# Cross-attention and a two-of-eight expert layer on one core: half the tokens through 15 sorted expert tiles, the other half dense

## The reference, cut to what matters

```
x   = x + xattn(layernorm(x), ctx)            # x (4, 256, 128), ctx (4, 1601, 128), one head of 128
x   = x + ffn(layernorm(x))

# ffn, per token (4 * 256 = 1024 tokens):
scores = softmax(flat @ router_weight.T + router_bias)        # 8 experts
topk_w, topk_idx = top_k(scores, 2)
gu   = einsum('th,ehn->ten', flat, gate_up_proj) + gate_up_bias   # (1024, 8, 512)
gate = minimum(gu[..., :256], 7);  up = clip(gu[..., 256:], -7, 7)
act  = (up + 1) * gate * sigmoid(1.702 * gate)
down = einsum('tei,eih->teh', act, down_proj) + down_bias         # (1024, 8, 128)
out  = sum over the two chosen experts of topk_w * down
```

## Time and profile before

| | |
|---|---|
| median of 3 runs | 157.16 us (156.94 to 157.22) |
| the profiled execution | 156.96 us |
| span of its trace | 155.2 us |
| TensorE busy | 149.2 us, 96% of the span |
| granted TensorE clock | 1.00 throughout |
| DMA queues | 10.69 MB, nearly all in the first fifth of the span |

### The profile page before, as it was taken

One profiled execution on the slowest core, in us unless ns is written; L12 is line 12 of the kernel. 1 busy time (PEld: TensorE's weight loads), 2 busy tenths in 40 slices (PEclk: granted clock), 3 DMA queues, 4 the chain that ended last, 5 costly groups with the idle time before them and its releaser, 6 DMA issues.

```text
span 155.2 us, 3023 instructions
## 1 busy us (share of the span) xinstructions
PE 149.2 (96%) x1004; PEld 136.0 (88%) x1004; DVE 103.2 (66%) x288; ACT 100.8 (65%) x205; POOL 49.8 (32%) x49
## 2 busy tenths in 40 slices
PE   7998799999999999999999999999999999999993
PEld 7988699999999999989988888788888888887892
DVE  0668958386859595963683899957654377552773
ACT  3183878657484736468866656957788677779450
POOL 1356529243505300210067643312333321233020
PEclk9999999999999999999999999999999999999999
DMA  4979999700000000000000000000000000000022
GB/s 116 371 292 404 388 401 384 225 1 4 0 2 0 4 0 0 4 0 2 0 0 4 0 0 0 0 4 0 2 0 0 0 0 0 0 4 0 4 68 68
DMA packets 5909, 10.69 MB, mean 69 GB/s; under 512 B 380, under 2 KB 3080, under 8 KB 5896
## 3 DMA queue, kind: packets, MB, share of 16 engines
q1 hardware_dynamic: 4968, 10.00, 17.9%
q10 hardware_dynamic: 928, 0.53, 1.2%
HBM read 10.00 MB, written 0.52 MB: 68 GB/s over the span
## 4 chain that ended last, share of the span: by engine, by line
PE 78%; DVE 10%; POOL 4%; ACT 3%; issue 3%; DVEq 0%
PE T L1147 14%; PE O L1041 13%; PE S L944 11%; PE S L946 10%; PE S L945 10%; PE T L1025 6%; PE S L951 3%; POOL ex L309 2%; DVE xT L847 2%; DVE up L838 1%; PE S L1147 1%; DVE w_lo L779 1%; DVE sc L631 1%; ACT pr L419 1%; POOL rstd L287 1%
## 5 line engine op out<-in xcount | busy, mean ns | idle before, releaser
L838 DVE TENSOR_SCALAR up<-up 128x512 f32<-128x512 f32 x32 | 13.9, 434 | 24.7 <-ACT up L504 24.7
L350 POOL TENSOR_TENSOR x<-x,xn 128x512 f32<-128x512 f32 x13 | 17.3, 1331 | 38.6 <-ACT xn L524 38.6
L427 ACT ACTIVATE pT<-T 128x512 f32<-128x512 f32 (+1 forms) x32 | 15.4, 513 | 18.4 <-PE T L1025 18.4
L524 ACT ACTIVATE xn<-T,w_scaled 128x128 f32<-128x128 f32 x56 | 16.1, 374 | 17.2 <-PE T L1147 14.1
L944 PE MATMUL S<-x_hi,w_hi 128*128 128x512 f32 x64 | 26.8, 419 | 0.2 <-DVE w_lo L779 0.2
L1041 PE MATMUL O<-pT,ctx_sb 128*128 128x128 f32 (+1 forms) x208 | 25.9, 275 | 0.2 <-ACT pT L427 0.2
L945 PE MATMUL S<-x_lo,w_hi 128*128 128x512 f32 x64 | 25.3, 395 | 0.0
L946 PE MATMUL S<-x_hi,w_lo 128*128 128x512 f32 x64 | 25.3, 395 | 0.0
L1041 PEld LDWEIGHTS O<-pT,ctx_sb 128*128 128x128 f32 (+1 forms) x208 | 24.6, 192 | 0.6 <-ACT pT L427 0.5
L631 DVE TENSOR_SCALAR_CACHE_REDUCE sc<-S,clip_hi 128x400 f32<-128x400 f32 (+1 forms) x32 | 18.9, 630 | 8.7 <-PE S L946 8.5
L498 ACT ACTIVATE keysT_sb<-S,gate_bias 128x512 f32<-128x512 f32 x32 | 22.7, 708 | 1.7 <-PE S L946 1.6
(11 more groups left out here) (127 smaller groups left out, 248.4 us busy)
## 6 DMA issues: line engine op xcount, KB each, us to landing
keysT_sb<-in_ctxT SPq DMA_DIRECT2D x3, 801.0 KB, 9.9
ctx_sb<-in_ctx SPq DMA_DIRECT2D x3, 768.0 KB
gu_sb<-in_gu SPq DMA_DIRECT2D x1, 2048.0 KB, 14.9
ctx_sb<-in_ctx SPq DMA_DIRECT2D x3, 256.0 KB, 4.5
x_sb<-in_x ACTq DMA_DIRECT2D x1, 384.0 KB, 5.0
keysT_sb<-in_ctxT SPq DMA_DIRECT2D x1, 289.0 KB, 5.5
out_x<-xn SPq DMA_DIRECT2D x1, 256.0 KB, 2.3
out_x<-xn SPq DMA_DIRECT2D x2, 128.0 KB, 1.8
```

The source lines that it names most:

```text
L350: nc.gpsimd.tensor_tensor(acc, acc, y_sb[:, k % 2, :], ALU.add).then_inc(y_added, 1)
L524: ins = nc.scalar.activation(y_sb[:, k % 2, t * DIM:(t + 1) * DIM], T[k % 2][:, t * DIM:(t + 1) * DIM], ACT.Copy, scale=w_scaled[:, bass.d ...
L838: nc.vector.tensor_scalar(up[:, k % 2, ih, :], up[:, k % 2, ih, :], 2.0 * LIMIT, 1.0 - LIMIT, ALU.min, ALU.add).then_inc(up_clipped, 1)
```

## The change

Batches 2 and 3 (512 tokens) stay dense: 8 steps instead of 16. Batches 0 and 1 (512 tokens, each with two experts, so 1024 rows) are sorted by expert into tiles of 128 rows, each tile of one expert. 1024 rows are 8 tiles, and 8 experts can leave up to 7 more partly filled: 15 tiles always, whatever the routing.

- During attention, the router results of batches 0 and 1 are ranked on VectorE (`rank_experts`), TensorE counts how many rows of each expert come before each token (`count_before`, 2 and 6 small matmuls), VectorE turns that into a row number (`find_rows`), and GpSimd scatters the normalised rows to DRAM (`send_rows`, 4 indirect DMAs a batch), with the place of its result as a 129th column. The DRAM area is filled with ones first (`blank_rows`, 2.6 MB). An indirect DMA with no use for its data goes first (`first_send`).
- Behind the last attention tile's router, VectorE computes from the counts which expert each tile belongs to and where its rows start (`compare_counts`, `tile_table`). SP reads each start into a register and loads the tile (15 loads). TensorE reads each tile's expert into a register (`load_expert`).
- A tile on TensorE: one transposition, a bias product of 16 rows by 512 columns, three products of 512 columns with the rows as stationary operand, two transpositions of the activations, and two float32 matmuls of 128 columns. ScalarE does four instructions a tile (128, 256, 256, 128 columns), VectorE three (128, 256, 256). GpSimd scatters each result (`send_result`), SP brings all of them back behind the last, and VectorE adds them with their weights (`sum_results`).
- All eight experts' weights are split ahead and kept, on ScalarE (`weights_hi`) and GpSimd (`weights_lo`, 8 subtractions of 128x512), instead of on VectorE one by one. They are loaded where the transposed keys lie, in three DMAs (`expert_weights`), each waiting for its keys' last reader.
- Expert 0 of the dense half is split in two items of 256 columns: batch 2 ahead of the tiles, batch 3 behind them. The other seven follow.
- The blank operand of the first matmuls is now `ones`, 1677 columns wide instead of 128.

```
+SPARSE = [0, 1]
+DENSE = [2, 3]
+RT = len(SPARSE) * TPB
+RTOK = RT * P
+SLOTS = RT * TOP_K + EXPERTS - 1
...
+            def expert_weights(k):
+                e0, n = W_PARTS[k]
+                sp.wait_ge(keys_lo_ready, (k + 1) * NCH)
+                sp.dma_start(keysT_sb[:, k, 0:n * 2 * HIDDEN].rearrange("p (e n) -> p e n", e=n),
+                             gu[e0:e0 + n].rearrange("e h n -> h e n")).then_inc(w_in[k], 16)
...
+            sp.wait_ge(first_row_ready, 1)
+            for i in range(SLOTS):
+                at = sp.value_load(first_row[0:1, i:i + 1], min_val=0, max_val=ROWS - P)
+                if i == 0:
+                    for s in range(len(SPARSE)):
+                        sp.wait_ge(rows_sent[s], 16 * TOP_K * TPB)
+                sp.dma_start(xt[:, i, :], xs[bass.ds(at, P), :]).then_inc(xt_in[i], 16)
...
+                pool.wait_ge(pads_in, 16)
+                pool.wait_ge(first_sent, 16)
+                pool.wait_ge(payload_copied, s + 1)
+                pool.wait_ge(row_ready, s + 1)
...
+                        nc.gpsimd.indirect_dma_start(xs[:, :], bass.IndirectOffsetOnAxis(ap=row_of[:, s, k:k + 1], axis=0),
...
+            def send_result(i):
+                pool.wait_ge(y_ready, i + 1)
+                nc.gpsimd.indirect_dma_start(yb[:, :], bass.IndirectOffsetOnAxis(ap=xt[:, i, DEST:DEST + 1].bitcast(I32), axis=0),
...
+            first_send()
             root2(0)
+            copy_payload(0)
             keys_lo(3, 0)
+            weights_lo(0)
+            weights_lo(1)
+            weights_lo(2)
             keys_lo(3, 1)
+            weights_lo(3)
             root2(1)
+            copy_payload(1)
+            send_rows(0)
+            weights_lo(4)
+            weights_lo(5)
             root2(2)
+            send_rows(1)
+            weights_lo(6)
+            weights_lo(7)
             root2(3)
...
+            for k in range(-2, SLOTS + 2):
+                if 0 <= k - 2:
+                    evict(k - 2)
+                if 0 <= k - 1 < SLOTS:
+                    copy_act(k - 1)
+                if k + 2 < SLOTS:
+                    split_rows(k + 2)
+                if 0 <= k + 1 < SLOTS:
+                    silu(k + 1)
...
+            def tile_table():
+                dve.wait_ge(counted, 1)
+                link(nc.vector.tensor_reduce(tiles_of[:], full[:], AX.X, ALU.add))
+                nc.vector.tensor_scalar(gap[:], tiles_of[:, 0:EXPERTS - 1], -float(P), float(RTOK), ALU.mult, ALU.add)
+                link(nc.vector.tensor_tensor(tiles_upto[:], upto[:], tiles_of[:].unsqueeze(1).to_broadcast([P, EXPERTS - 1, EXPERTS]),
+                                             ALU.mult))
+                link(nc.vector.tensor_reduce(last_of[:], tiles_upto[:], AX.X, ALU.add))
+                shape = [P, SLOTS, EXPERTS - 1]
+                link(nc.vector.tensor_tensor(passed[:], tile_no[:].unsqueeze(2).to_broadcast(shape),
+                                             last_of[:].unsqueeze(1).to_broadcast(shape), ALU.is_ge))
+                link(nc.vector.tensor_reduce(expert_no[:], passed[:], AX.X, ALU.add))
+                link(nc.vector.tensor_tensor(passed[:], passed[:], gap[:].unsqueeze(1).to_broadcast(shape), ALU.mult))
+                link(nc.vector.tensor_reduce(skipped[:], passed[:], AX.X, ALU.add))
+                nc.vector.scalar_tensor_tensor(first_row[:], tile_no[:], float(P), skipped[:], ALU.mult,
+                                               ALU.add).then_inc(first_row_ready, 1)
+                nc.vector.tensor_scalar(expert_at[:], expert_no[:], float(P), None, ALU.mult)
+                nc.vector.tensor_scalar(bias_pick[:], expert_no[0:BIAS_ROWS, :], bias_expert[:, 0:1],
+                                        None, ALU.is_equal).then_inc(table_ready, 1)
...
-            nc.vector.memset(act_odd[:, 0:P], 0.0).then_inc(blank_ready, 1)
+            nc.vector.memset(ones[:], 1.0).then_inc(blank_ready, 1)
             nc.vector.memset(inv_sum[:, 0:1], 0.0).then_inc(pad_ready, 1)
...
+            def gate_up(i):
+                if i == 0:
+                    load_expert(0)
+                    pe.wait_ge(bias_ready, 1)
+                    pe.wait_ge(w_lo_ready, EXPERTS)
+                    pe.wait_ge(d_silu_ready, 2)
+                pe.wait_ge(xt_lo_ready, i + 1)
+                if i >= 2:
+                    pe.wait_ge(up_ready, i - 1)
+                cols = bass.ds(expert[i], P)
+                dst = GU[i % 2][:].rearrange("p (c n) -> p c n", c=WIDTH)
+                nc.tensor.matmul(GU[i % 2][:], bias_pick[:, i:i + 1].to_broadcast([BIAS_ROWS, P]), bias_parts[:],
+                                 start=True, stop=False)
+                nc.tensor.matmul(dst, xt_hi[:, i % 2, :], w_hi[:, :, cols], start=False, stop=False)
+                nc.tensor.matmul(dst, xt_hi[:, i % 2, :], w_lo[:, :, cols], start=False, stop=False)
+                nc.tensor.matmul(dst, xt_lo[:, i % 2, :], w_hi[:, :, cols], start=False, stop=True).then_inc(gu_done, 1)
+                if i + 1 < SLOTS:
+                    load_expert(i + 1)
...
+            dense_gate_up(0, 1, 0)
+            dense_gate_up(0, 1, 1)
+            for k in range(-2, SLOTS + 1):
+                if k + 2 < SLOTS:
+                    transpose_rows(k + 2)
+                if 0 <= k + 1 < SLOTS:
+                    gate_up(k + 1)
+                if 0 <= k - 1:
+                    down(k - 1)
+                if k == SLOTS - 1:
+                    dense_gate_up(1, 0, 0)
+                    dense_gate_up(1, 0, 1)
+                if 0 <= k < SLOTS:
+                    transpose_act(k)
+                if k == SLOTS - 1:
+                    dense_gate_up(1, 1, 0)
+                if k == 1:
                     transpose_x2(last)
-                    routed_bias(0)
+                if k == X2_LAST:
                     router(last)
...
+            dense_gate_up(1, 1, 1)
+            dense_gate_ups(2)
+            for e in range(EXPERTS - 2):
+                dense_down(e)
+                if e in (1, 3):
+                    routed_bias(e // 2)
+                dense_gate_ups(e + 3)
+                if e in (0, 2):
+                    transpose_weights(e // 2)
+            dense_down(EXPERTS - 2)
+            dense_down(EXPERTS - 1, tiles_apart=True)
 
```

918 lines of the change are left out of this document (591 added, 327 removed).

## The result

The changed kernel takes **168.98 us** (median of 4 runs, 168.82 to 169.37) against 157.16 before: a ratio of 1.076, 95% interval 1.074 to 1.078. I had forecast 154.8, range 150 to 162, and slower only with a chance of 0.38. The profiled execution has a span of 167.3 us where the sum gave 153.0.

What follows compares the result with a forecast made beforehand. TensorE, busy 96% of the span, was taken as the bound. Span: 155.2 - 11.0 - 1.4 + 1.3 + 0.9 + 1.1 + 5.0 + 1.4 + 0.5 = 153.0; plus 1.8 gives 154.8 us, range 150.0 to 162.0.

Steps and rivals of the forecast that it cites:

- start: Kernel start: TensorE's first record waits for the memset of the wider block of ones, +1.3 us.
- GpSimd ahead of root2(1): Attention, batch 1: weight subtractions queued before GpSimd's root make VectorE's normalisation and TensorE wait, +1.1 us, bounds 0 and 2.
- Counting: TensorE's queue: the 2 and then 6 narrow matmuls of `count_before` add 0.9 us.
- Between attention and the tiles: Between last router and first tile: TensorE idle 5.0 us for table, register read and row load, bounds 3.5 and 8.
- dense steps: Expert layer: eight of sixteen dense steps of 4.59 us go, -36.7 us.
- The sorted rows come late: Rival: batch 2 of scatters lands after SP's first register; rows 3.9 us late, 158.7 us; chance 0.09.
- The waits are smaller: Rival: start, root2, gap and tile waits each cost less than forecast, 150.8 us; chance 0.21.
- The rate of the tiles: Tile stretch: ScalarE and VectorE keep up with TensorE, waits of 0.09 us a tile, +1.4 us, bounds 0.3 and 4.5.
- Tiles: TensorE's work per tile, 1.71 us with all four 512-column products at 0.233; fifteen tiles +25.7 us.
- The clock: Rival: TensorE slows down behind its 5 us idle time, up to 4 us lost, 157 to 159 us; chance 0.13.
- A slower tile rate: Rival: register loads on SP and TensorE delay each tile by 0.5 us, +7.5, 162.3 us; chance 0.19.
- The saving of 1.4 us in stalls: Just behind attention: weight splits leave VectorE and routing moves beside the tiles, -1.4 us, bounds 0 to -2.

Runs made afterwards that it cites:

- e5_rows128: The changed kernel with each tile's bias product on 128 rows, zeros behind the sixteen: 162.22 us, ratio 1.035.
- e15_rows64: e13_apart with its bias product on 64 rows instead of 128: 157.13 us, one run.
- e13_apart: Changed kernel with 128-row bias product, early tile table, small reorderings, filled idle times, and GpSimd's weight parts 2-5 waiting for VectorE's batch 1 choice: 153.36 us, ratio 0.978.
- e2_fixed: The changed kernel with each tile's expert on TensorE a constant instead of a loaded register: 167.60 and 168.54 us at clock 0.959, 179.4 and 179.5 at 0.894.
- e16_change_apart: The changed kernel with only GpSimd's weight parts 4 and 5 made to wait for VectorE's batch 1 choice: 167.64 us at clock 0.959, others 176.43 to 176.71.
- e10_more: Changed kernel with 128-row bias product, early tile table, moved GpSimd weight parts, later batch 3 router, earlier row addresses and other small reorderings: 157.92 us, ratio 1.007.
- e14_apart_unfilled: e13_apart without the products that fill TensorE's short idle times ahead of the first tile: 153.98 us, ratio 0.982.

## Why the prediction was wrong

**Right, or nearly.** The *start*: +1.3 forecast, first scores at 11.27 instead of 10.21, +1.1. *GpSimd ahead of root2(1)*: +1.1 forecast, 0.98 measured at 55.44, with VectorE waiting as described. *Counting*: the six narrow matmuls of batch 1 take from 67.60 to 68.26, the two of batch 0 take 0.22, together +0.9. *Between attention and the tiles*: 4.17 us and then 0.69 + 0.59 of idle time, 5.45 against 5.0. The *dense steps* are 4.55 where no bias work lies between them (150.72 to 155.27). *The sorted rows come late* is refuted: a scatter keeps GpSimd for 1.0 us (1.46 the one beside VectorE's pass over 1601 columns), the next follows 1.28 later, and the load waited for the table. *The waits are smaller* is refuted as well.

**Right by luck.** The last router but one starts at 77.33, where the terms put it at 77.8. But 12 products of 512 columns stood ahead of it before (67.40 to 71.17), and now 6 of 256 do (73.19 to 73.97): some 2 us of the dense work that the sum takes off at the end leave here. Without luck the router would have had to come at about 75.8. Attention lost some 1.5 us more than the terms say, 1.05 of them ahead of the count of batch 1.

**The step that failed** is "The rate of the tiles" with the sum of one tile under "Tiles": three transpositions, "four products of 512 columns (0.233 each)" and two float32 matmuls make 1.71, plus 0.09 of waits. From the first bias product to the first product of a whole dense step (126.28) pass 40.4 us, where the terms (15 x 1.80, batch 3's transposition and router 0.9, the second item 1.4, the turn 0.5) give 29.9. That is 10.5 of the 14.3 us between the forecast span of 153.0 and 167.3.

- *One of the four products has 16 rows.* I priced it as its neighbours. The turn costs 0.3 to 0.38 us a tile, 15 x 0.30 = 4.5 us (e5_rows128; e15_rows64 for 64 rows). I picked no row that shows it, but the trace before has two such places, each with four products of 8 rows, and the one at 142.78 gives 0.38: this term could have been read before the change was made. The Trainium skill (TensorEngine Tiling (Array Packing), "Key Properties") states that changing the tiling mode drains TensorE. The same page ("Available Configurations") lists 64 rows as another mode than 128; it does not say that an ordinary product of few rows is such a change. The weight loads that start only with their products, and the 65 rows that cost nothing, agree with it. The rule is one that speaks against this change, and it was missing from the sum.
- *The clock.* The sum had nothing for it. It was a rival, with 0.13, "157 to 159 us", and its mechanism holds. Five periods from the first bias product take 15.84 us; in e13_apart, at full clock and 128 rows, they take 10.29. Less five turns (1.5 to 1.9) that is 3.7 to 4.0 us, so its price, 2 to 4, holds too. By the rule of the Trainium skill that the prediction cites there the first tiles would show 0.5, and the trace agrees: they show 0.50 up to about 95.7. What failed is taking it as an alternative to slower tiles: it came on top of them.
- *Single waits.* 1.06 us for batch 3's router and 0.65 + 0.30 at the last two tiles come on top of the period, where the transition to the dense steps had 0.5: 1.5 more.
- *A slower tile rate* was a rival with 0.19 and the right sign, but its cause, the register load, is refuted by e2_fixed: the period did not move.

**A term that was missing.** Nothing in the sum stood for GpSimd's eight subtractions beside VectorE. I had noted that GpSimd's root loses time beside VectorE's long pass and not turned the thought round. It cost 1.05 us directly in the changed kernel, and e16_change_apart takes them out. In the improved ones it cost 3.7 us, clock included: the first tile transposition stands at 79.72 in e10_more and at 75.98 in e14_apart_unfilled.

**Still open.** In the dense stage the last activation waits put 0.8 us on the tail: from the start of the last 32 down records (159.82, before 148.55) to the end of the span are 7.48 us instead of 6.65, with 0.51 of idle time on TensorE. e10_more took that idle time away. The saving of 1.4 us in stalls was not tested by itself, and about 1 us of the 14.3 is put down to nothing. What exactly ends a stretch at the lower clock is open: by their mean clocks the kernels with 16 rows were there for up to some 40 us, those with 128 rows for at most some 10, but no run isolates why. How GpSimd's parts can hold a comparison that is listed as starting 0.6 us ahead of them is open too.

Where the 16.0 us between the spans of the changed kernel and e13_apart lie: 4.2 up to the last router but one (77.33 to 73.17), 3.6 from there to the first bias product (85.91 and 78.15), and the rest, 8.2, behind it, nearly all in the tiles.

## What to carry to other kernels

In a tight run of matmuls on 128 rows, don't leave single ones on 64 rows or fewer (64, 16 and 8 were measured); pad them with zeros: on 128 rows the bias product was cheaper than on 16 or 64. If there are several, put them side by side: four of 8 rows paid for going there and back only once. Work given to an idle GpSimd is not free: look for VectorE operations that read SBUF beside it and shift it by a wait, not by a guess in its queue. And price an idle time of TensorE with what the lower clock takes afterwards: here 2.0 us of it cost 3.7 in all. The idea of the change was sound: with these repaired, it beats the kernel before by 2.2%.
